# Linear attention inside a three-layer decoder kernel: sums G and folded weights M as fp16 high and low parts, with three fp16 products in place of one fp32 product

## The chip, the core and the metric

The kernel runs on one core of a Trainium2 chip. The core has a matrix engine (PE, TensorE), with its weight loads shown apart as PEld, a vector engine (DVE), a scalar engine (ACT), GpSimd (POOL) and a queue engine (SP) that issues DMA transfers. The metric is the device time in microseconds (us) of one whole execution.

## What is computed

128 sequences of 64 tokens, 128 wide, pass through linear attention, cross attention and a feed-forward layer, each followed by a layer norm. The change is in the linear attention, which the reference writes so (biases left out here):

```python
q_prime = exp(einsum('bnhd,df->bnhf', x @ Wq, wq_feat))          # 16 heads, 32 features
k_prime = exp(einsum('bnhd,df->bnhf', x @ Wk, wk_feat))
D_inv   = 1.0 / (einsum('bnhf,bhf->bnh', q_prime, k_prime.sum(axis=1)) + 1e-06)
context = einsum('bnhf,bnhd->bhfd', k_prime, x @ Wv)
out     = einsum('bnhf,bhfd,bnh->bnhd', q_prime, context, D_inv).reshape(b, n, H * DH) @ Wproj
```

The kernel regroups it. For a sequence b it forms G = x^T k_prime, which is 128 x 512 (all heads side by side). For each head h it multiplies the 32 columns of G by M_h = Wv_h Wproj_h, a 128 x 128 matrix that is folded once. The result C (128 rows of features for four heads at a time, four times 128 columns) is what q_prime, already scaled by D_inv, is multiplied with.

## The kernel before

The 128 sequences are worked in 16 groups of 8 (s = 0 to 15). All five engines run hand-written programs. Each walks through the same list of steps, PLAN, and does its own part of each step, so PLAN alone sets the order on every engine: HEAD is a prologue, PERIOD is one round of 86 steps that repeats 14 times with different groups in flight at once (`@2` is a step of the group two before), TAIL drains the rest. An engine executes in order: a step that waits holds up all that stands behind it on that engine.

The PE writes into eight banks of PSUM. Every step that needs a bank takes the next in rotation, so the step that stands eight bank uses later has to wait until this bank has been read out ("emptied"). Evictions are by ACT or DVE. For some steps a `+` in PLAN says that ACT does it, otherwise DVE.

The steps that matter here, for one group:

- `k0` to `k3`: k_prime for two sequences each. PE makes three fp16 products (L270 to L272), ACT takes exp into kp (L569). `q0` to `q3`: the same for q_prime into qT (L278 to L280, L576).
- `g0` to `g7`: G of one sequence. PE L320, one fp32 product of 64 rows by 512 columns (two records in the trace). It is copied out of its bank into one of four buffers GT: in PERIOD g0, g1 and g2 by ACT (L588, seen as L549) and the other five by DVE (L846). g4 to g7 reuse the buffers of g0 to g3, so their copies wait until c0 to c3 have been computed.
- `c0` to `c7`: C of one sequence. PE L330, 16 fp32 products, one for each head, with 32 columns of GT as the weights and 128 columns of Mh streamed. Four heads in turn go to the four 32-column strips of the array. One fp32 product is two matmul records and two weight-load records in the trace. C is copied into Cb, by ACT for c0, c4 and c7, by DVE for the others (L852).
- `ks`, `kst`, `dT`, `bc0` to `bc3`: the denominators. PE L287, L295, L305, L313. The step `dT` also needs DVE (De, Dv) and POOL (Dblk, L1056); `bc` scales qT on DVE (L838).
- `o0` to `o3`: PE L343 and L347, then DVE adds the residual (L860) and the layer norm follows: statistics (L867, L874) on DVE, `st1` to `st3` on POOL (L1061, L1064), `ap1` to `ap3` on DVE (L880).
- Cross attention: `kproj` and `qproj` evicted by ACT (L616, L620; L631, L633) and DVE (L887), `score` reduced to maxima by DVE (L897), `rows` (PE L409), `prob` (PE L421, L428; ACT L662), `pv` (PE L443; DVE L809), `oturn` (PE L451; DVE L905, L912), `cs` (a split into high and low parts by ACT L673 and POOL L1139, then a transposing DMA L1219), `proj` (PE L471 to L473; DVE L920).
- Feed-forward: `ap2` also splits x2 on POOL (L1090, L1092) for a transposing DMA; `up` (PE L491, L492; ACT Gelu L691), `stat` on DVE and POOL, `gs`, `gh`, `gl` (POOL L1106, ACT L709, POOL L1111), `down` (PE L511, L512; DVE L971).

In PERIOD the first half of G and C stands as `g0+ g1+ g2+ g3 ap2@3 down2@4 k3 ... prob0@2 prob1@2 st3@4 ap1@1 ap3@4 c0+ c1 pv0@2 ... c2`, the second half as `q2 cs1@2 oturn1@2 q3 g4 g5 g6 gs2@3 gl0@3 g7 gh1@3 qproj@1 gl1@3 kproj@1 c3 dT c4+ c5 c6 gs3@3 c7+ proj0@2 csplit proj1@2`.

## Time and profile before

| | |
|---|---|
| median of 3 runs | 674.9 us (671.55 to 675.94) |
| span of the profiled execution | 673.3 us |
| PE busy | 645.5 us (96%) |
| PEld busy | 455.3 us (68%) |
| DVE busy | 535.4 us (80%) |
| ACT busy | 437.5 us (65%) |
| POOL busy | 448.9 us (67%) |
| share of the chain that ended last: PE | 66% |
| same: POOL, DMA, DVE, issue, ACT | 12%, 8%, 6%, 4%, 2% |
| granted clock of the PE, mean | 0.997 |

Busy time counts the time in which at least one instruction of the engine was running. Matmuls overlap, so the number that matters for the PE is the distance from start to start, and an engine at 96% is not proved to be the limit by that number. The chain that ended last is followed back from the last instruction: at each step to what released it. "Idle before" and the brackets [... <-engine] in the rows give how long an engine stood still before an instruction and what it waited for.

### The profile page before, as it was taken

To read this page: it belongs to the slowest core of one execution; us is meant where nothing else is said; L and a number is where in the kernel's file an instruction comes from. 1 tells how busy PE (TensorE), PEld (TensorE's weight loads), DVE (VectorE), ACT (ScalarE), POOL (GpSimd) and SP (SyncE) were. 2 spreads that over 40 slices of the span, in tenths; PEclk is the share of its full clock that TensorE was granted. 3 is DMA by queue.
4 is the path that set the end of the run, shared out by engine and by line. 5 is a ranking of instruction groups with operands and counts; after the bars stand their busy time and mean duration, and the time that the engine had idled before them with its cause. 6 is when DMAs were issued, how large, how long until landed. Compare 5 with 4: busy or idle time off the path is not lost.

```text
span 673.3 us, 30461 instructions
## 1 busy us (share of the span) xinstructions
PE 645.5 (96%) x13160; PEld 455.3 (68%) x13160; DVE 535.4 (80%) x1485; ACT 437.5 (65%) x755; POOL 448.9 (67%) x495
## 2 busy tenths in 40 slices
PE   9999999999999989999999999999999999999684
PEld 6766767666766766676666667667666767667473
DVE  1656678788888878897788888878888888887787
ACT  3546465849578574947848494875849486777462
POOL 3233134867769586776959687795977779786652
PEclk9999999999999999999999999999999999999998
DMA  8102121262452434353343527336343634352300
GB/s 333 34 18 34 36 50 52 37 109 50 88 92 50 113 50 97 50 104 74 50 113 50 96 52 103 74 51 112 60 90 55 121 50 66 65 81 36 65 34 33
DMA packets 117816, 49.26 MB, mean 73 GB/s; under 512 B 108337, under 2 KB 108722, under 8 KB 117554
## 3 DMA queue, kind: packets, MB, share of 16 engines
q1 hardware_dynamic: 117682, 47.31, 36.7%
q8 instruction: 104, 1.70, 1.1%
q14 instruction: 30, 0.25, 0.1%
HBM read 16.88 MB, written 4.19 MB: 31 GB/s over the span
## 4 chain that ended last, share of the span: by engine, by line
PE 66%; POOL 12%; DMA 8%; DVE 6%; issue 4%; ACT 2%; SPq 2%; POOLq 0%; DVEq 0%
PE bank L330 12%; PE bank L347 7%; PE bank L320 6%; PE bank L443 4%; PE bank L428 4%; DMA cT<-cs 4%; PE bank L400 3%; POOL gall L1106 3%; DMA gT<-gs 2%; POOL rstd L1064 2%; PE bank L343 2%; DVE st L867 2%; PE bank L270 2%; PE bank L287 2%; PE bank L313 2%
## 5 line engine op out<-in xcount | busy, mean ns | idle before, releaser
L330 PEld LDWEIGHTS bank<-Mh,GT 128*32 128x32 f32 x4096 | 110.4, 110 | 23.9 <-issue 18.1
L330 PE MATMUL bank<-Mh,GT 128*32 128x128 f32 x4096 | 125.7, 273 | 0.5 <-issue 0.4
L897 DVE TENSOR_REDUCE mx<-bank 128x8 f32<-128x512 f32 x128 | 78.2, 682 | 13.4 <-PE bank L400 13.4
L1106 POOL TENSOR_TENSOR gall<-gall,lnr 128x512 f32<-128x512 f32 x56 | 71.3, 1283 | 20.7 <-DVE st L867 20.7
L846 DVE COPY GT<-bank 128x512 f32<-128x512 f32 x78 | 51.0, 688 | 36.3 <-PE bank L330 19.6
L662 ACT ACTIVATE PT<-bank 128x512 f32<-128x512 f32 x128 | 64.6, 622 | 14.1 <-PE bank L428 14.0
L1064 POOL TENSOR_TENSOR rstd<-ve,mhalf 128x4 f32<-128x4 f32 x64 | 66.6, 1041 | 5.3
L347 PE MATMUL bank<-Cb,qT 128*64 128x128 f32 x1024 | 67.2, 273 | 0.0
L1111 POOL TENSOR_TENSOR gs<-gall,gs 128x512 f16<-128x512 f32 x56 | 64.1, 1165 | 1.5 <-ACT gs L709 1.5
L320 PE MATMUL bank<-kp,xs 64*128 64x512 f32 x256 | 64.0, 616 | 0.0
L549 ACT ACTIVATE Mrow<-bank 64x128 f16<-64x128 f32 x16 | 4.3, 271 | 83.7 <-PE bank L409 83.7
L852 DVE COPY Cb<-bank 128x512 f32<-128x512 f32 x80 | 52.6, 673 | 7.6 <-PE bank L330 7.6
L347 PEld LDWEIGHTS bank<-Cb,qT 128*64 128x64 f32 x1024 | 58.4, 137 | 0.2 <-issue 0.2
L576 ACT ACTIVATE qT<-bank,qb 128x512 f32<-128x512 f32 x64 | 43.5, 683 | 12.1 <-PE bank L280 11.7
L880 DVE TENSOR_SCALAR x<-x,mv,rstd 128x128 f32<-128x128 f32 x128 | 49.6, 451 | 1.5 <-POOL rstd L1064 0.9
L1041 POOL TENSOR_TENSOR x<-x,bias 128x512 f32<-128x512 f32 x32 | 40.7, 1273 | 6.6 <-PE bank L481 4.4
L620 ACT ACTIVATE Kg<-bank,bkm,small 128x512 f32<-128x512 f32 x64 | 44.8, 801 | 0.0
L838 DVE TENSOR_TENSOR qT<-qT,bank 128x512 f32<-128x512 f32 x64 | 39.7, 682 | 6.2 <-PE bank L313 5.4
L569 ACT ACTIVATE kp<-bank 128x512 f32<-128x512 f32 x64 | 36.6, 597 | 11.9 <-PE bank L272 11.0
L867 DVE BATCH_NORM_STATS2 st<-gall 128x6 f32<-128x512 f32 x64 | 39.5, 680 | 5.2 <-ACT gall L691 5.0
L1027 POOL CAST xh<-xT 128x512 f16<-128x512 f32 x16 | 9.8, 610 | 50.6 <-DMA xT<-in_xT 50.6
L691 ACT ACTIVATE gall<-bank 128x512 f32<-128x512 f32 x64 | 33.4, 601 | 13.6 <-PE bank L492 13.6
(198 smaller groups left out, 1640.9 us busy)
## 6 DMA issues: line engine op xcount, KB each, us to landing
xT<-in_xT SPq DMA_DIRECT2D x16, 256.0 KB, 3.3
xs<-in_x_nat SPq DMA_DIRECT2D x16, 256.0 KB, 3.2
cxT<-in_cxT SPq DMA_DIRECT2D x16, 256.0 KB, 3.8
out_y<-yo SPq DMA_DIRECT2D x15, 256.0 KB, 2.0
Qm<-in_Wvp SPq DMA_DIRECT2D x1, 1024.0 KB, 7.4
gT<-gs SPq DMA_TRANSPOSE x56, 3.7
gall<-in_Wff SPq DMA_DIRECT2D x1, 768.0 KB, 10.0
small<-in_small SPq DMA_DIRECT2D x1, 523.0 KB, 8.6
```

The source lines that it names most:

```text
L320: e.matmul(bk[:, :], xs[s % 2][r0:r0 + 64, tile(t)], kp[r0:r0 + 64, tile(t, 512)], start=True, stop=True).then_inc(done, 1)
L330: m = e.matmul(bk[32 * j:32 * j + 32, tile(g_)], GT[b % 4][:, tile(hh, 32)], Mh[:, tile(hh)], start=True, stop=True)
L347: m = e.matmul(bk[64 * bb:64 * bb + 64, 0:128], qT[:, g_ * 512 + b * 64:g_ * 512 + b * 64 + 64], Cb[b][:, tile(g_)], start=False, stop=(g_ ...
L662: e.activation(PT[tp][:, tile(j, 512)], bank[uses["prob", s, i][0]][:, :], ACT.Exp, scale=SM).then_inc(emptied("prob", s, i)[0], 1)
L846: e.tensor_copy(GT[b % 4][:, :], bank[uses["g", s, b][0]][:, :]).then_inc(emptied("g", s, b)[0], 1)
L852: e.tensor_copy(Cb[b][:, :], bank[uses["c", s, b][0]][:, :]).then_inc(emptied("c", s, b)[0], 1)
L867: e.bn_stats(st[k][:, 6 * t:6 * t + 6], x[t]).then_inc(s_st[k], 1)
L880: e.tensor_scalar(x[:, tile(t)], x[:, tile(t)], mv[k][:, 2 * t:2 * t + 1], rstd[k][:, t:t + 1], ALU.subtract, ALU.mult).then_inc(s_ln[k], 1)
L897: e.tensor_reduce(mx[s % 2][:, c0:c0 + 8], bank[uses["score", s, i][0]][:, :].rearrange("p (n k) -> p n k", k=64), AX.X, ALU.max).then_inc ...
L1064: e.tensor_tensor(rstd[k][:, :], ve[k][:, :], mhalf[:, :], ALU.pow).then_inc(s_rstd[k], 1)
L1106: e.tensor_tensor(g[t][:, :], g[t][:, :], lnr[:, :], ALU.mult).then_inc(s_gs, 1)
L1111: e.tensor_tensor(gs[t % 2][:, 512:1024], g[t][:, :], gs[t % 2][:, 0:512], ALU.subtract).then_inc(s_gl, 1)
```

## The change

M is now kept as two fp16 matrices. ACT writes the bank times 16 (1/GS, GS = 1/16) into Mh, DVE writes the bank times 16 less Mh into Ml. G is kept the same way: for every g step ACT writes G/16 into one of four buffers Gh, and then DVE reads the same bank again and writes the remainder into Gl. The two scale factors cancel in the product. The bank is given free by DVE. So ACT now evicts all eight g of a group (three before) and DVE also works on all eight (five before), each after ACT. The wait for the buffer (`filled("c", ...)`) stands on ACT. The `+` after a g step no longer means anything; PLAN is not touched.

In cmat, 48 fp16 products take the place of 16 fp32 ones: for each set of four heads Gh by Mh, Gl by Mh and Gh by Ml, summed in PSUM.

```diff
-        Mh = sb("Mh", 2048)
+        Mh, Ml = sb("Mh", 2048, F16), sb("Ml", 2048, F16)
...
-                for hh in range(H):
-                    g_, j = hh // 4, hh % 4
-                    m = e.matmul(bk[32 * j:32 * j + 32, tile(g_)], GT[b % 4][:, tile(hh, 32)], Mh[:, tile(hh)], start=True, stop=True)
+                for g_ in range(4):
+                    for G, M in ((Gh, Mh), (Gl, Mh), (Gh, Ml)):
+                        for j in range(4):
+                            hh = 4 * g_ + j
+                            m = e.matmul(bk[32 * j:32 * j + 32, tile(g_)], G[b % 4][:, tile(hh, 32)], M[:, tile(hh)], start=(G is Gh and M is Mh), stop=(M is Ml))
                 m.then_inc(done, 1)
...
# ACT, gmat, now called for every g
-                copy("g", s, b, GT[b % 4][:, :])
+                w.wait_ge(*filled("g", s, b))
+                e.activation(Gh[b % 4][:, :], bank[uses["g", s, b][0]][:, :], ACT.Copy, scale=GS).then_inc(s_gth, 1)
...
# DVE, gmat, now called for every g
-                if b >= 4:
-                    w.wait_ge(*filled("c", s, b - 4))
-                elif s > 0:
-                    w.wait_ge(*filled("c", s - 1, b + 4))
-                w.wait_ge(*filled("g", s, b))
-                e.tensor_copy(GT[b % 4][:, :], bank[uses["g", s, b][0]][:, :]).then_inc(emptied("g", s, b)[0], 1)
+                w.wait_ge(s_gth, 8 * s + b + 1)
+                e.scalar_tensor_tensor(Gl[b % 4][:, :], bank[uses["g", s, b][0]][:, :], GS, Gh[b % 4][:, :],
+                                       ALU.mult, ALU.subtract).then_inc(emptied("g", s, b)[0], 1)
```

Three places show where the instructions stand. On ACT, at the second half of G in a steady round, before the change: the exp of q3, the high part gs1 of the feed-forward, and the evictions of qproj and kproj follow each other.

```order
L576 ACTIVATE qT<-bank5,qb 128x512 [waits s_bank5_full]
L709 ACTIVATE gs1<-gall 128x512 [waits s_g3_transposed,s_g_scaled]
L631 ACTIVATE Qu<-bank2,small2 128x512 [waits s_bank2_full]
L633 ACTIVATE Qm1<-bank2,bqm,small2 128x512 x2
L616 ACTIVATE Km1<-bank3,small2 128x512 [waits s_bank3_full]
L620 ACTIVATE Kg<-bank3,bkm,small2 128x512 x4
```

The same place after the change:

```order
L581 ACTIVATE qT<-bank5,qb 128x512 [waits s_bank5_full]
L594 ACTIVATE Gh0<-bank6 128x512 [waits s_bank6_full]
L594 ACTIVATE Gh1<-bank7 128x512 [waits s_bank7_full]
L594 ACTIVATE Gh2<-bank0 128x512 [waits s_bank0_full,s_bank2_full]
L594 ACTIVATE Gh3<-bank1 128x512 [waits s_bank1_full,s_bank4_full]
L715 ACTIVATE gs1<-gall 128x512 [waits s_g3_transposed,s_g_scaled]
L637 ACTIVATE Qu<-bank2,small2 128x512 [waits s_bank2_full]
L639 ACTIVATE Qm1<-bank2,bqm,small2 128x512 x2
L622 ACTIVATE Km1<-bank3,small2 128x512 [waits s_bank3_full]
L626 ACTIVATE Kg<-bank3,bkm,small2 128x512 x4
```

Four evictions now stand ahead of gs1 and the two projections, and the last (Gh3) also waits for bank4, the bank of c3, to be full.

On DVE, the same place before the change (GT0 to GT3 are g4 to g7, Qm1 is DVE's half of the qproj eviction):

```order
L912 TENSOR_TENSOR cn1<-bank4,rs1 128x16x2x8 [waits s_c_lo,s_rs]
L846 COPY GT0<-bank6 128x512 [waits s_bank6_full]
L846 COPY GT1<-bank7 128x512 [waits s_bank7_full]
L846 COPY GT2<-bank0 128x512 [waits s_bank0_full]
L846 COPY GT3<-bank1 128x512 [waits s_bank1_full,s_bank4_full]
L887 TENSOR_SCALAR Qm1<-bank2,small2 128x512 [waits s_Q_masked]
```

After it (this copy of the place has the bank numbers of another group):

```order
L922 TENSOR_TENSOR cn1<-bank7,rs1 128x16x2x8 [waits s_c_lo,s_rs]
L855 SCALAR_TENSOR_TENSOR Gl0<-bank1,Gh0 128x512 [waits s_G_hi]
L855 SCALAR_TENSOR_TENSOR Gl1<-bank2,Gh1 128x512 [waits s_G_hi]
L855 SCALAR_TENSOR_TENSOR Gl2<-bank3,Gh2 128x512 [waits s_G_hi]
L855 SCALAR_TENSOR_TENSOR Gl3<-bank4,Gh3 128x512 [waits s_G_hi]
L897 TENSOR_SCALAR Qm0<-bank5,small2 128x512 [waits s_Q_masked]
```

Four copies became four subtractions; what they wait for is now ACT.

On PE, one c step (c0 of a group) after the change. Before, it was one row of 16 products, `MATMUL bank<-Mh,GT 32x128 x16`. Here are its first seven rows, of which the last six are two of the four sets:

```order
L334 MATMUL bank5<-Mh,Gh0 32x128 [waits s_bank5_empty]
L334 MATMUL bank5<-Mh,Gh0 32x128 x3
L334 MATMUL bank5<-Mh,Gl0 32x128 x4
L334 MATMUL bank5<-Ml,Gh0 32x128 x4
L334 MATMUL bank5<-Mh,Gh0 32x128 x4
L334 MATMUL bank5<-Mh,Gl0 32x128 x4
L334 MATMUL bank5<-Ml,Gh0 32x128 x4
```

Each c step now has twelve rounds of four products; the four of a round go to four different strips of the array.

## Rows read from the trace of the kernel before

**Rows 1.** Windows: length; busy us of PE, PEld, DVE, ACT, POOL; clock, DMA.

```profile
107.60:574.20 466.60, 458.25 (x9703) 321.79 (x9701) 392.59 (x1081) 325.30 (x556) 353.22 (x383) 1.00 0.42 75
...
301.90:341.60 39.70, 38.57 (x812) 27.18 (x811) 32.60 (x91) 26.86 (x46) 29.39 (x32) 1.00 0.43 71
...
459.70:497.50 37.80, 37.80 (x813) 26.80 (x811) 32.53 (x92) 26.96 (x46) 29.08 (x32) 1.00 0.44 74
```

**Rows 2.** Timeline of PE, second half of C: start us, length us, instruction, count.

```profile
323.83 1.08 PE L330 MATMUL bank<-Mh,GT 128*32 128x128 f32 x32
324.73 1.08 PE L305 MATMUL bank<-qT,KSz 128*32 128x64 f32 x64
325.62 3.83 PE L330 MATMUL bank<-Mh,GT 128*32 128x128 f32 x128
329.38 0.23 PE L471 MATMUL bank<-xWh,cT 128*128 128x128 f16 x1
...
329.73 0.22 PE L471 MATMUL bank<-xWh,cT 128*128 128x128 f16 x1
```

**Rows 3.** Groups by line: instructions, busy us, mean ns of one, idle before.

```profile
L751 DVE TENSOR_TENSOR Wkfl<-bank,Wkfh 128x512 f16<-128x512 f32 x1 | 0.7, 692 | 6.9 <-ACT Wkfh L553 6.9
L887 DVE TENSOR_SCALAR Qm<-bank,small 128x512 f32<-128x512 f32 x32 | 24.4, 804 | 5.7 <-ACT Qm L633 5.7
L553 ACT ACTIVATE Wkfh<-bank 128x512 f16<-128x512 f32 x1 | 0.6, 597 | 6.3 <-PE bank L210 6.3
```

**Rows 4.** Timeline of DVE over one round.

```profile
304.21 0.69 DVE L846 COPY GT<-bank 128x512 f32<-128x512 f32 x1 [0.77 <-PE bank L320]
304.82 1.11 DVE L880 TENSOR_SCALAR x<-x,mv,rstd 128x128 f32<-128x128 f32 x4
...
310.71 1.12 DVE L880 TENSOR_SCALAR yo<-yo,mv,rstd 128x128 f32<-128x128 f32 x4 [0.91 <-POOL rstd L1064]
...
315.53 0.69 DVE L809 COPY OT<-bank 128x512 f32<-128x512 f32 x1 [1.24 <-PE bank L443]
316.70 2.47 DVE L867 BATCH_NORM_STATS2 st<-gall 128x6 f32<-128x512 f32 x4 [0.47 <-ACT gall L691]
...
321.12 0.42 DVE L912 TENSOR_TENSOR cn<-bank,rs 128x256 f32<-128x256 f32 x1
...
324.98 0.69 DVE L846 COPY GT<-bank 128x512 f32<-128x512 f32 x1 [1.35 <-PE bank L330]
...
336.30 4.88 DVE L897 TENSOR_REDUCE mx<-bank 128x8 f32<-128x512 f32 x8 [1.25 <-PE bank L400]
```

**Rows 5.** Timeline of ACT over the same round.

```profile
303.24 1.57 ACT L549 ACTIVATE GT<-bank 128x512 f32<-128x512 f32 x3 [0.72 <-PE bank L320]
...
321.58 0.42 ACT L673 ACTIVATE cs<-cn 128x256 f16<-128x256 f32 x1
321.91 0.67 ACT L576 ACTIVATE qT<-bank,qb 128x512 f32<-128x512 f32 x1
322.48 0.62 ACT L709 ACTIVATE gs<-gall 128x512 f16<-128x512 f32 x1
323.29 0.69 ACT L631 ACTIVATE Qu<-bank,small 128x512 f32<-128x512 f32 x1 [0.19 <-PE bank L376]
...
325.77 2.80 ACT L620 ACTIVATE Kg<-bank,bkm,small 128x512 f32<-128x512 f32 x4
```

**Rows 6.** Timeline of PE over the same round.

```profile
302.08 1.99 PE L320 MATMUL bank<-kp,xs 64*128 64x512 f32 x8
...
335.19 1.99 PE L400 MATMUL bank<-Kg,Qu 32*64 32x256 f32 x64 [0.20 <-ACT kp L569]
```

**Rows 7.** Timeline of POOL, the step ap2 and the root of st3.

```profile
305.99 0.61 POOL L1090 CAST x2s<-x 128x512 f16<-128x512 f32 x1 [0.96 <-DVE x L880]
...
309.56 1.12 POOL L1064 TENSOR_TENSOR rstd<-ve,mhalf 128x4 f32<-128x4 f32 x1
```

**Rows 8.** Who waited for whom: us in total, times, longest us.

```profile
PE bank L471 <- DMA cT<-cs: 5.5, 6, 1.7
```

More of the change, by code:

```diff
@@ L557, in mh @@
                     o = Mh[:, :].rearrange("p (c k a n) -> p c k a n", c=2, k=4, a=2)[:, c // 2, :, c % 2, :]
-                    copy("mh", 0, c, o, shape="p (k n) -> p k n")
+                    w.wait_ge(*filled("mh", 0, c))
+                    e.activation(o, bank[uses["mh", 0, c][0]][:, :].rearrange("p (k n) -> p k n", k=4), ACT.Copy, scale=1 / GS).then_inc(s_mhh, 1)
             def nbeta_():
@@ L756, in xw, with mh @@
                 e.tensor_tensor(xWl[:, :], xWall, xWh[:, :], ALU.subtract).then_inc(s_xwl, 1)
+            def mh(c2):
+                for c in range(2 * c2, 2 * c2 + 2):
+                    hi, lo_ = [v[:, :].rearrange("p (c k a n) -> p c k a n", c=2, k=4, a=2)[:, c // 2, :, c % 2, :] for v in (Mh, Ml)]
+                    w.wait_ge(s_mhh, c + 1)
+                    e.scalar_tensor_tensor(lo_, bank[uses["mh", 0, c][0]][:, :].rearrange("p (k n) -> p k n", k=4), 1 / GS, hi,
+                                           ALU.mult, ALU.subtract).then_inc(emptied("mh", 0, c)[0], 1)
             def sel_():
```

18 lines of the change are left out of this document (12 added, 6 removed).

## The prediction, made before the changed kernel was run

> **What bounds the kernel now.** I read the windows first. Between 107.6 and 574.2 us twelve rounds repeat, 466.6/12 = 38.9 us each, and the PE is busy in 458 of those 467 us [rows 1]. One round (459.7 to 497.5) has the PE busy for all of its 37.8 us; I take that as the PE's own work in a round, so an average round holds 1.1 us of stray PE waits. In the same stretch DVE is busy 392.6/12 = 32.7 us a round and ACT 27.1. So the PE is the bound, and a shorter PE program shortens the kernel only until another chain of waits is longer. The second view is the timeline of one round (301.9 to 341.6), engine by engine, because it shows how far the others are from being the bound: DVE stands still for 1.24 us before the pv copy, 1.35 us before the last g copy and 1.25 us before the score maxima, each time for the PE [rows 4].
>
> **PE: the c steps.** Four c steps in a row start at 325.62 and the next step starts at 329.38: 3.76/4 = 0.94 us each, and the single one before them took 324.73 - 323.83 = 0.90 [rows 2]. That is 32 matmul records of 128 columns in 0.90 us, 28 ns a record, where four records of different strips run side by side. New: 48 records, each with half the work of an old record (one pass over 128 fp16 columns; an fp32 record makes two passes, which I read from the row of L305: 64 records of 64 fp32 columns take 325.62 - 324.73 = 0.89 us, 13.9 ns each, half as long for half the columns). 128 columns once are as much as 64 columns twice, so 13.9 ns x 48 = 0.67 us; with the same small loss between steps 0.69. A c step gains 0.90 - 0.69 = 0.21 to 0.25 us, I take 0.22; 8 in a round gain 1.8 us, 128 in the kernel 28 us. Bounds: no better than 0.25 x 128 = 32 us; at the other end, if a record costs 28 ns whatever it does, a c step takes 48 x 28 = 1.34 us and loses 0.44.
>
> The Trainium skill, TensorEngine Tiling, section Instruction Overhead, puts about 60 cycles on every matmul, however short; at 2.4 GHz 48 of them would be an estimated 1.2 us a step, a loss of 0.3 where the row gives a gain. The row of L305, 13.9 ns a record in this same four-strip form, disagrees with that rule as a floor for tiled matmuls, and the sum goes by the row.
>
> **ACT and DVE: durations.** The low part on DVE reads PSUM and an fp16 tile and writes fp16. The nearest row is the same split of a weight, L751, 692 ns [rows 3] against 0.69 us for the plain copy [rows 4]; the dearest form, with two scalar columns, took 804 ns [rows 3]. Mine has a constant, so 0.69; back to back such instructions start every 0.60 us (eight in 4.88) [rows 4]. ACT's fp16 eviction is 597 ns [rows 3], and three in a row start every 0.49 us [rows 5]. Per round ACT does five more (2.5 us), DVE three more (1.8 us). DVE goes to 34.5 us of work, ACT to 29.6, the PE to 37.8 - 1.8 = 36.0. By work alone the PE would still be the bound and the kernel would be 28 us shorter. But the new work is in chains, and I walk one round to see what is late next. I hold the PE's g0 at 302.08 [rows 6].
>
> 1. First half of G. ACT copies from 303.24, now four: done at 303.24 + 3 x 0.49 + 0.60 = 305.3, just when it used to start the exp of k3, so ACT loses nothing. DVE begins at 303.9 (first high part done, and it was idle), subtracts four times by 0.60, and is free at 306.3. Before, it had one copy and began ap2 at 304.82 [rows 4]. DVE is 1.46 us late.
> 2. ap2 feeds POOL, which did nothing else then: it had waited 0.96 us for it [rows 7]. Its split, bias and root run in series to 309.56 + 1.12 = 310.68, and DVE waited 0.91 us for that before ap3 [rows 4]. All of it moves by 1.46: ap3 starts at 312.17. Five copies later (c1, OT, KS, c2, OT) DVE reaches the statistics at 312.17 + 1.04 + 5 x 0.60 = 316.2, against 316.70. The 1.24 us for which it waited for pv swallow the delay, since the PE is not behind: prob1 starts 0.55 late (its banks wait for down3 on DVE) and three c steps give 0.66 back. From here to the last cn DVE was busy throughout: cn ends at 321.0 instead of 321.54.
> 3. ACT: cs1 at 321.1, q3 at 321.4, then the four high parts from 322.0, step 0.49. The last waits for c3. With the PE about 1.3 us ahead by then (up no longer waits for a late pv, and the c steps are shorter), c3 is full near 323.4 and ACT reaches that copy at 323.45: no wait. gs1 at 323.95, Qu at 324.5 instead of 323.29 [rows 5], all evictions of the projections 1.2 us late, and the bank of kproj is free at 329.8 instead of 325.77 + 2.80 = 328.57.
> 4. PE: it would reach proj at 326.7, with c4 to c7 done. proj0 waits for the transposed cT and for DVE's share of qproj's bank (about 328.1); it waited for that DMA 6 times already [rows 8], and the same POOL and DMA work still stands ahead of it. proj1 waits for kproj's bank, 329.85. So about 3 us of PE waits take the place of the 1.8 us saved, and of the other time that the PE had won.
> 5. From the start of proj1 to score the PE took 335.19 - 329.73 = 5.46 us [rows 2, 6]; about 0.36 of it were waits, 0.20 for the exp of k0 [rows 6] and the rest my reading of small gaps at down and score, and both go since ACT and the DMAs are relatively earlier. So score starts at 329.85 + 5.10 = 334.95, 0.24 earlier than in this round, and the maxima on DVE with it.
>
> The round closes 0.24 us earlier than this one did, which was 39.70 us [rows 1]: 39.46. That is 0.58 more than the average of 38.88. Now DVE, POOL, ACT, and the PE from proj to o, are one ring: a stray delay on it counts, where the PE alone had 1.1 us. This round already has the usual ones of DVE and POOL in it; I allow 0.2 us more. **Sum:** 12 x (0.58 + 0.2) = +9.4 us. The c steps of the first two groups (before 107 us) stand where DVE and ACT have little to do: 2 x 1.8 = -3.6 us. In the last 99 us I give nothing either way: the gain of two groups' c steps against 3 more DVE instructions each. 673.3 + 9.4 - 3.6 = 679.1 us for the profiled execution, whose span is 1.6 us under the median of the runs: 680.7. I say 680.
>
> **Rivals.** *The PE stays the bound* (faster). For it: I count ACT's and DVE's work at its place in one round that happened to be long; if one of the waits in steps 1 to 3 is covered more than I think, each us off the ring is a us off the round until the PE's 36.0. Against it: the ring has no large slack left that I can find. All the way it is 645 us; halfway (a ring of 37.8 us) it is 673.3 - 12 x 1.1 - 3.6 = 656.5, and 658 for the runs.
>
> *ACT stands at the last high part* (slower). If the PE is not ahead at c3, so that it is full at 325.0 as before and not at 323.4, ACT's g7 copy ends at 325.6, all evictions behind it come another 1.6 us late, proj1 too, and the round is 39.5 + 1.6 = 41.1: 2.2 + 0.2 over the average, 12 x 2.4 - 3.6 = +25, or 700 for the runs. It decides from the point where c3 is full later than 323.45 on this clock. For it: the PE's lead of 1.3 us at g4 comes mostly from waits, not from work. Half as late gives 690.
>
> *The small matmuls cost a slot each* (slower; the change then does not do what it says). At 28 ns a record the PE needs 37.8 + 8 x 0.44 = 41.3 us a round, 2.4 over the average in 12 rounds, and 3.5 in each of the four groups at the ends: 673.3 + 29 + 14 = 716. In rows: this needs L305 to be no guide for fp16. With the 60 cycles of the Trainium skill's rule it would be about 702 as an estimate.
>
> **Chances.** My forecast (a ring of 39.0 to 40.2 us, 671 to 689 by the same sum) 0.55; the PE or a shorter ring 0.20; ACT's stand 0.20; slots 0.05. About 1% is what a measurement of this kernel can tell from no change, 668 to 682. The faster rival lies below that but for its upper end, 0.18. Slower takes the last two and a third of the forecast, 0.42. The same: 0.40. Range: 662 to 695 leaves out the lower half of the first rival (0.1) and the far end of the slow ones (0.1).
>
> **What would show it.** c steps of about 0.67 to 0.69 us from start to start; the low part on DVE at 0.69 us, the high part at 0.60. DVE starts ap2 about 4.2 us after the PE's g0 (2.74 before). PE waits of 2 to 3 us a round at proj (L475 to L477 of the new file), released by ACT's Kg or the cT DMA, where there were none or little; PE busy near 90%. If PE stays at 96% and the c steps are short, the ring was shorter than I counted. If c steps take over 0.9 us, the slots rival holds. If ACT idles before Gh for the PE's c, it is ACT's stand. What would make it wrong most easily is step 2, the order in which DVE's wait for pv and POOL's chain cover each other, since the whole delay of 1.46 us is hidden there.

## The result, and the profile after

The changed kernel takes **727.3 us** (median of 4 runs, 725.2 to 729.1) against 675.4 us for the kernel before on the same chip. The ratio is 1.079, 95% interval 1.076 to 1.082. It is slower by 52 us where I had predicted 680 and a range that ended at 695. The chip has a second, slower state that some executions fall in, and all times and ratios below are of the others.

| | before | after |
|---|---|---|
| span of the profiled execution | 673.3 us | 725.3 us |
| PE busy, matmuls | 645.5 us (96%), 13160 | 634.7 us (88%), 15208 |
| DVE busy, instructions | 535.4 us (80%), 1485 | 566.2 us (78%), 1539 |
| ACT busy, instructions | 437.5 us (65%), 755 | 473.6 us (65%), 833 |
| start to start over 12 rounds | 466.6 / 12 = 38.88 us | 504.8 / 12 = 42.07 us |
| ahead of these rounds | 107.6 us | 119.1 us |
| behind them | 99.1 us | 101.4 us |
| granted clock of the PE, mean | 0.997 | 0.994 |

Of the 52 us, 38.2 come from the twelve rounds, 11.5 from the stretch ahead of them and 2.3 from the end. The window over the twelve rounds, in the columns of [rows 1]:

```profile
119.10:623.90 504.80, 449.40 (x11239) 306.30 (x11237) 413.69 (x1117) 352.83 (x616) 353.90 (x383) 1.00 0.39 70
```

Against the first row of [rows 1], the PE's busy time fell by 8.9 us in twelve rounds, less than half of the 12 x 1.8 = 21.6 that I had predicted. And the PE now stands still for 504.8 - 449.4 = 55.4 us, 4.6 us a round, where it stood still for 8.4 us in all. The granted clock of this window is 1.00, so it is not a slower clock. Who is waited for stands in the waits (us in total, times, longest):

```profile
PEld bank L334 <- issue: 62.2, 87, 2.2
DVE Gl L855 <- ACT Gh L594: 41.2, 47, 2.5
PE bank L334 <- issue: 35.8, 27, 2.0
ACT Gh L594 <- PE bank L334: 16.8, 17, 2.4
PEld bank L475 <- ACT Kg L626: 9.0, 9, 1.5
```

L334 is the c step, L594 ScalarE's high part, L855 VectorE's low part, L626 the eviction Kg, L475 the step proj. The largest PE wait is not for another engine. "Issue" means that nothing in the profile released it. Before, the weight loads of the c step had stood 18.1 us in this way, and its matmuls 0.4. The groups by line show that each new operation lasts as long as I had taken it to (busy us, mean ns; then idle before):

```profile
L855 DVE SCALAR_TENSOR_TENSOR Gl<-bank,Gh 128x512 f16<-128x512 f32 x128 | 81.3, 685 | 41.3 <-ACT Gh L594 41.2
L334 PE MATMUL bank<-Mh,Gh 128*32 128x128 f16 x2048 | 94.7, 220 | 14.9 <-issue 13.1
L594 ACT ACTIVATE Gh<-bank 128x512 f16<-128x512 f32 x128 | 68.1, 602 | 34.7 <-PE bank L322 17.7
```

**Inside the c steps.** The PE's timeline in the round that begins with g0 at 413.18 us, from the second (c5) of four c steps in a row back to back to the end of the fourth (c7) (start us, length us, instruction, count, idle before):

```profile
437.97 0.23 PE L334 MATMUL bank<-Mh,Gh 128*32 128x128 f16 x4
438.03 0.23 PE L334 MATMUL bank<-Mh,Gl 128*32 128x128 f16 x3
...
439.42 0.23 PE L334 MATMUL bank<-Mh,Gl 128*32 128x128 f16 x1 [1.16 <-issue]
439.42 0.28 PE L334 MATMUL bank<-Ml,Gh 128*32 128x128 f16 x4
...
441.10 0.27 PE L334 MATMUL bank<-Ml,Gh 128*32 128x128 f16 x4
441.16 0.23 PE L334 MATMUL bank<-Mh,Gh 128*32 128x128 f16 x3
...
443.43 0.23 PE L334 MATMUL bank<-Mh,Gh 128*32 128x128 f16 x1 [2.05 <-issue]
...
443.71 0.23 PE L475 MATMUL bank<-xWh,cT 128*128 128x128 f16 x1
```

Groups of four matmuls start 0.055 us apart, and then, in the middle of a group of four whose operands have long been there, the engine stops for 1.16 and for 2.05 us. Nothing has a semaphore there. The c steps c4 to c7 need 192 x 13.9 ns = 2.7 us when nothing is in the way. Here they take from 437.30 to 443.71, 6.4 us, 1.6 each.

The clue is in where it stops. I counted the PE's instructions (weight loads and matmuls) from the start of the program. The four matmuls of this round after which it stops inside a step have the numbers 18161, 18416, 18926 and 19182: 255, 510 and 256 apart. The profile's DMA part has a queue that carries instructions. This is its row before, after, and in two experiments of the next section (e7 has 32 PE instructions in a c step where before has 64 and after 96; e4 has 128):

```profile
q8 instruction: 104, 1.70, 1.1%
```

```profile
q8 instruction: 120, 1.97, 1.1%
```

```profile
q8 instruction: 88, 1.44, 1.0%
```

```profile
q8 instruction: 136, 2.23, 1.2%
```

Blocks of 1.70 MB / 104 = 16 KB. With two instructions to a matmul the four programs have 26320, 30416, 22224 and 34512 PE instructions. Divided by 256 that is 102.8, 118.8, 86.8 and 134.8, each time 1.2 blocks less than the row: one block is 256 PE instructions. In the trace's DMA records the blocks of the round above start at 420.60, 424.11, 428.08, 436.69, 440.71 and 445.52. The stops end at 422.96, 426.52, 439.42 and 443.43, 2.4 to 2.7 us behind the start of a block. Two starts are never less than 3.29 us apart in the whole run (3.24 in the kernel before). With 3.4 us to a block, near the shortest, the PE is given an instruction every 13.3 ns, or 27 ns for a matmul with its weight load. **A c step of 96 instructions is then given in 1.28 us, though it is done in 0.67.** In the round above the blocks are further apart, 3.97 and 4.02 us, which makes 15.7 ns an instruction and 1.5 us a step, near the 1.6 that c4 to c7 take. Before, a c step had 64 instructions, given in 0.85 us at 3.4 us a block and done in 0.90 [rows 2]: just supplied. That is the reading that I had missed.

### The profile page after: what moved, and what is told of

It is laid out like the page before. It is cut to its first block, busy times and chain, and to the rows that moved or that the text cites. A ratio compares the mean times of both kernels' runs of the same rounds, so it can differ in the third digit from the quotient of the medians.

```text
span 725.3 us, 34692 instructions
## 1 busy us (share of the span) xinstructions
PE 634.7 (88%) x15208; PEld 436.6 (60%) x15208; DVE 566.2 (78%) x1539; ACT 473.6 (65%) x833; POOL 449.5 (62%) x495
## 4 chain that ended last, share of the span: by engine, by line
PE 65%; DVE 11%; ACT 9%; issue 9%; POOL 4%; DMA 1%; SPq 0%; POOLq 0%; DVEq 0%; ACTq 0%
PE bank L334 9%; PE bank L351 7%; PE bank L322 6%; PE bank L447 4%; DVE Gl L855 4%; PE bank L404 4%; ACT Kg L626 3%; PE bank L315 2%; PE bank L432 2%; PE bank L347 2%; PE bank L289 2%; PE bank L455 2%; PE bank L272 2%; ACT Qm L639 2%; DVE x L890 2%
## 5 line engine op out<-in xcount | busy, mean ns | idle before, releaser
L855 DVE SCALAR_TENSOR_TENSOR Gl<-bank,Gh 128x512 f16<-128x512 f32 x128 | 81.3, 685 | 41.3 <-ACT Gh L594 41.2
L334 PE MATMUL bank<-Mh,Gh 128*32 128x128 f16 x2048 | 94.7, 220 | 14.9 <-issue 13.1
L334 PE MATMUL bank<-Ml,Gh 128*32 128x128 f16 x2048 | 94.4, 219 | 13.7 <-issue 13.7
L334 PE MATMUL bank<-Mh,Gl 128*32 128x128 f16 x2048 | 93.9, 219 | 9.0 <-issue 9.0
L594 ACT ACTIVATE Gh<-bank 128x512 f16<-128x512 f32 x128 | 68.1, 602 | 34.7 <-PE bank L322 17.7
L334 PEld LDWEIGHTS bank<-Mh,Gh 128*32 128x32 f16 x2048 | 62.8, 97 | 33.2 <-issue 32.1
L334 PEld LDWEIGHTS bank<-Ml,Gh 128*32 128x32 f16 x2048 | 63.5, 97 | 15.6 <-issue 15.5
L334 PEld LDWEIGHTS bank<-Mh,Gl 128*32 128x32 f16 x2048 | 62.8, 97 | 14.5 <-issue 14.5
L447 PE MATMUL bank<-PT,Vblk 128*32 128x64 f32 x2048 | 39.2, 220 | 12.3 <-issue 11.8
```

Source lines behind the costliest of these rows:

```text
L334: m = e.matmul(bk[32 * j:32 * j + 32, tile(g_)], G[b % 4][:, tile(hh, 32)], M[:, tile(hh)], start=(G is Gh and M is Mh), stop=(M is Ml))
L447: m = e.matmul(bk[32 * j:32 * j + 32, tile(2 * g_ + t2, 64)], V3[s % 2][:, 32 * tp + 16 * t2 + hh, :], PT[tp][:, c0:c0 + 64], start=True, ...
L594: e.activation(Gh[b % 4][:, :], bank[uses["g", s, b][0]][:, :], ACT.Copy, scale=GS).then_inc(s_gth, 1)
L855: e.scalar_tensor_tensor(Gl[b % 4][:, :], bank[uses["g", s, b][0]][:, :], GS, Gh[b % 4][:, :], ALU.mult, ALU.subtract).then_inc(emptied("g ...
```

## The experiments

Rounds are counted from the step `rows` of one group to the next, over the same twelve rounds. "Stops" are the distances of two matmuls of one step that are 0.15 us or more over the usual one with no wait between them, counted between 105 and 700 us, and their sum in us; where nothing stands I did not count. "PE instr." is the number of PE instructions in a c step. Each ratio is to runs of the kernel before that were made together with that kernel's (medians 673.9 to 676.3 us).

| kernel | us | ratio [95%] | round | stops, sum | PE instr. | evictions of G |
|---|---|---|---|---|---|---|
| before | 675.4 | 1 | 38.88 | 3, 2.1 | 64 | one |
| after | 727.3 | 1.079 [1.076, 1.082] | 42.06 | 35, 44.4 | 96 | two |
| e1_high_product_only | 711.9 | 1.054 [1.047, 1.061] | 41.21 | 11, 10.9 | 32 | two |
| e2_products_without_evictions | 711.3 | 1.054 [1.049, 1.058] | 40.98 | 36, 49.7 | 96 | one |
| e3_evictions_without_products | 707.8 | 1.050 [1.045, 1.054] | 41.09 | 10, 7.1 | 64 | two |
| e4_fp32_products_cut_in_two | 766.0 | 1.136 [1.129, 1.143] | 45.16 | 47, 72.8 | 128 | one |
| e5_c_steps_spread | 743.4 | 1.101 [1.094, 1.107] | 43.84 | 11, 11.2 | 96 | one |
| e6_weights_split_only | 674.2 | 0.998 [0.995, 1.001] | 39.00 | 24, 24.9 | 64 | one |
| e7_one_fp16_product | 666.7 | 0.988 [0.983, 0.994] | 38.45 | 8, 7.2 | 32 | one |
| e8_last_g_behind_projections | 727.8 | 1.075 [1.071, 1.079] | 42.71 | | 64 | two |
| e9_first_half_evictions | 685.4 | 1.017 [1.013, 1.021] | 39.76 | 11, 7.4 | 64 | two for g0 to g3 |
| e10_second_half_evictions | 698.1 | 1.035 [1.030, 1.039] | 40.29 | 5, 4.2 | 64 | two for g4 to g7 |
| e11_one_product_shorter_ring | 676.4 | 1.005 [1.000, 1.011] | 39.67 | | 32 | one |
| e12_before_shorter_ring | 676.2 | 1.003 [0.999, 1.006] | 38.83 | 7, 3.6 | 64 | one |
| e13_before_pool_ring_shorter | 706.6 | 1.043 [1.040, 1.047] | 41.38 | 9, 6.9 | 64 | one |
| e14_one_product_pool_ring_shorter | 710.1 | 1.050 [1.045, 1.054] | 41.99 | | 32 | one |
| e15_after_pool_ring_shorter | 746.5 | 1.101 [1.096, 1.106] | 43.86 | 38, 50.4 | 96 | two |

### The parts of the change apart

**e1** keeps the evictions and leaves out the two low products:

```diff
-                    for G, M in ((Gh, Mh), (Gl, Mh), (Gh, Ml)):
+                    for G, M in ((Gh, Mh),):
```

> The changed kernel with one product in a c step (Gh by Mh) in place of three; both low products are left out, while ACT and DVE still make all high and low parts. The PE executes 32 instructions (weight loads and matmuls) a c step, where the changed kernel has 96 and the kernel before 64. Theory A, instruction supply: in the changed kernel the PE stands still inside its c steps because its instructions arrive in blocks of 256 no faster than one in 3.47 us (13.6 ns an instruction); with 32 instructions that ends, no step has a gap inside it, and what is left is the ring of ACT, DVE and POOL of the prediction. If that ring is 39.1 us a round as I counted, 670 to 680 us; if it has slack, down to 640. Theory B, the ring alone costs the 50 us: about 720 still. Theory C, an fp16 product in four strips is slow by itself (a slot each): in between, about 675, with c steps of 0.45 us.

**e2** keeps the three products' form and count, but G is evicted once, as before, and all three use the same tiles (the low parts are left out):

```diff
-                    for G, M in ((Gh, Mh), (Gl, Mh), (Gh, Ml)):
+                    for n in range(3):
...
-                e.scalar_tensor_tensor(Gl[b % 4][:, :], bank[uses["g", s, b][0]][:, :], GS, Gh[b % 4][:, :], ...
+                e.tensor_scalar(GT[b % 4][:, :], bank[uses["g", s, b][0]][:, :], 2.0 ** -4, None, ALU.mult) ...
```

> The kernel before with its own evictions (one fp16 copy of G, by the engine that did it before; M as one fp16 copy) and 48 fp16 products a c step, three times the same pair, so that the PE does exactly what it does in the changed kernel while ACT and DVE do what they did before (the sum is three times the high product, no low parts). Theory A: the gaps inside c steps are all there, 690 to 720 us. Theory B: the PE gains 0.22 us a c step and nothing else changes, 645 to 655 us. Theory C: c steps are long evenly, not by gaps; about 700.

**e3** is the opposite: the changed evictions, and on the PE the program of the kernel before, one fp32 product, of the remainder (the high product is left out):

```diff
-        Gh, Gl, Cb = [sb(f"Gh{i}", 512, F16) for i in range(4)], [sb(f"Gl{i}", 512, F16) for i in range(4)], ...
+        Gl, Cb = [sb(f"Gl{i}", 512) for i in range(4)], ...
+        Gh = [v[:, 256:512].bitcast(F16) for v in Gl]
...
-                    for G, M in ((Gh, Mh), (Gl, Mh), (Gh, Ml)):
+                    for G, M in ((Gl, Mh),):
```

> The changed evictions of G (ACT writes a high part for all eight, then DVE works on all eight, the wait for the buffer on ACT) with the PE program of the kernel before, 16 fp32 products a c step. DVE writes the low part as fp32 and the PE multiplies that (M is one fp32 copy as before), so the high product is left out. Theory B, the ring with the PE late at c3: a round of 41 us, about 700 us or more. Theory A: the PE's own work and its instruction supply are those of before, and the evictions cost what is not hidden: 675 to 690.

Measured: the products alone cost 2.10 us a round (e2), the evictions alone 2.21 (e3), and both together 3.18. Counted in the traces from the start of one matmul to the start of the next, the c steps take 8.26 us a round in e2 and 8.27 after, against 7.25 before, and the pv steps, which follow c steps and were not changed, 3.19 and 2.94 against 2.13. For e2 these two make up 2.07 of its 2.10 us.

So there are **two losses of about the same size**, and they cover each other for 1.1 us: a PE that is held up comes later to the place where it would have waited for ScalarE. I read this overlap from the shrunken waits (below, step 4) and not from a run of its own. The stretch ahead of the rounds ends at 117.6 us in e2 and 111.7 in e3, against 107.6 before and 119.1 after. The 11.5 us lost there are thus mostly the products': that is where c steps stand close together and little else runs.

The share of the evictions is a plain chain. e3's ScalarE and PE in one round, whose g0 is at 400.91 us:

```profile
423.53 0.60 ACT L594 ACTIVATE Gl<-bank 128x512 f16<-128x512 f32 x1 [0.94 <-PE bank L335]
...
427.01 2.81 ACT L626 ACTIVATE Kg<-bank,bkm,small 128x512 f32<-128x512 f32 x4
```

```profile
428.49 0.22 PE L478 MATMUL bank<-xWl,cT 128*128 128x128 f16 x1
429.87 0.23 PE L476 MATMUL bank<-xWh,cT 128*128 128x128 f16 x1 [1.17 <-ACT Kg L626]
```

The last high part (g7) stands and waits for c3, which must have freed its tile. Behind it stand the evictions of the projections, the last of them Kg, which frees the bank of kproj, and PE's proj1 waits for that. In each of the twelve rounds ScalarE waits 0.9 us there (10.7 us in twelve), and the PE then waits for Kg, 13.7 us in twelve. This is the rival that I had called "ACT stands at the last high part": it had the last high part end 1.6 us late, at 325.6 on the prediction's clock, and e3's ends at 325.3. It said a round of 41.1, and e3's is 41.09, but that the two agree so closely is in part luck: the rival put all of its 2.2 us on the second half of G, and e9 and e10 below find 0.88 us for the first half and 1.41 for the second.

e1 has in a c step half the PE instructions of e3, with the same evictions, and its round is the same, 41.21, where I had expected 670 to 680 us in all. Its PE is not the bound: it is busy for 86% of the span. It no longer waits at c3, and in the round that is looked at below, at step 5, it gives about 1.4 us back to a slower clock. That this holds for every round I have not shown.

### Is it the supply of instructions?

**e4** takes the kernel before and cuts each fp32 product of 128 columns in two of 64, nothing left out. The columns to be multiplied are the same, the instructions twice as many:

```diff
-                    m = e.matmul(bk[32 * j:32 * j + 32, tile(g_)], GT[b % 4][:, tile(hh, 32)], Mh[:, tile(hh)], start=True, stop=True)
+                        for n in range(2):
+                            m = e.matmul(bk[32 * j:32 * j + 32, 128 * g_ + 64 * n:128 * g_ + 64 * n + 64], GT[b % 4][:, tile(hh, 32)], ...
```

> The kernel before with one edit: each fp32 product of a c step (128 columns) is cut in two of 64 columns. The columns streamed and all results are the same, but a c step has 128 PE instructions in place of 64. Nothing changes on ACT and DVE. Theory A: 128 x 13.6 ns = 1.74 us a c step when the supply binds, against 0.90: gaps inside c steps at multiples of 256 instructions, 710 to 760 us. Theories B and C: 64-column fp32 records take 13.9 ns each in L305, so a c step stays at 0.90 us, 675 us.

It is the slowest kernel of all, 766 us and 45.16 a round, 6.3 over before and more than the 710 to 760 us expected. The c steps take 11.83 us a round from start to start, 4.58 more than before, and the pv steps 1.20 more. In its timeline the stops stand as they do after:

```profile
416.54 0.84 PE L332 MATMUL bank<-Mh,GT 128*32 128x64 f32 x45
418.78 1.99 PE L332 MATMUL bank<-Mh,GT 128*32 128x64 f32 x128 [1.39 <-issue]
422.52 0.69 PE L332 MATMUL bank<-Mh,GT 128*32 128x64 f32 x34 [1.75 <-issue]
```

They come after the instructions 18694, 18950, 19460 and 19716: 256, 510 and 256 apart. The 128 matmuls between two stops are 256 instructions, one block.

**e5** is e2 with the c steps spread over the round, so that they no longer follow each other closely (low parts left out, as in e2):

```diff
-k0 k1 ... k3 down3@4 ab2@3 q0 prob0@2
-prob1@2 st3@4 ap1@1 ap3@4 c0+ c1 pv0@2 ... q3 g4 ... c3 dT c4+ c5 c6 gs3@3 c7+ proj0@2 csplit proj1@2 vproj@1 xb gh2@3 ...
+k0 k1 ... k3 c0+ down3@4 ab2@3 q0 c1 prob0@2
+prob1@2 st3@4 ap1@1 ap3@4 pv0@2 ... q3 g4 ... c3 dT c4+ gs3@3 proj0@2 csplit proj1@2 c5 vproj@1 xb c6 gh2@3 ... bc1 c7+ bc2
```

> The run e2 (48 products a c step three times the same pair, the evictions of the kernel before) with nothing changed but places in the repeating part of the plan: c0, c1, c2 and c5, c6, c7 no longer stand in a row beside pv and dT but between steps with few and long instructions (k, q, up, proj, vproj, bc). Number and kind of all instructions are the same on every engine. Instruction supply: the blocks of 256 can now be fetched while the PE works, most gaps inside steps go, and of the 37 us that e2 is over the kernel before most come back: 660 to 685 us. If the gaps belong to the products and not to how dense they stand, it stays at 711, or is worse because evictions are out of their tuned places.

The stops fall from 36 (49.7 us) to 11 (11.2 us), with the same 96 instructions in a c step. That is what the supply says and what a cost in each matmul would not. The time did not follow, though: 743.4 us where 660 to 685 was expected, and slower than e2. The evictions of the c banks now stand where VectorE is needed for other things (it waits 43.8 us for the PE's c steps, 7.6 in the kernel before, and GpSimd 88.4 us for VectorE's statistics, 38.3 before). So the stops speak for the cause, the time by itself does not, and the spreading is no remedy.

**e6** splits only the weights: two fp16 products, G in a single fp16 part (G's low part left out), evictions as before. It has as many PE instructions as the kernel before, and half of its columns in the c step:

```diff
+                for g_ in range(4):
+                    for n, M in enumerate((Mh, Ml)):
...
+                            m = e.matmul(bk[32 * j:32 * j + 32, tile(g_)], GT[b % 4][:, tile(hh, 32)], M[:, tile(hh)], start=(n == 0), stop=(n == 1))
```

> The kernel before with M as fp16 high and low parts (split once in the prologue), G as one fp16 copy made by the engine that made it before, and two fp16 products a c step, 64 PE instructions as in the kernel before (the low part of G is left out). By columns a c step is half as long, 0.45 us, and a round has 3.6 us less PE work. Without a supply limit: about 645 us. With one (256 instructions take at least 3.47 us): c4 to c7 have the 256 instructions they always had and still need about 3.5 us, against 3.6 before; 660 to 675 us, and the gaps inside steps are back.

**e7** has one fp16 product (all low parts left out), evictions as before:

```diff
-        Mh = sb("Mh", 2048)
+        Mh = sb("Mh", 2048, F16)
...
-        GT, Cb = [sb(f"GT{i}", 512) for i in range(4)], ...
+        GT, Cb = [sb(f"GT{i}", 512, F16) for i in range(4)], ...
```

> The kernel before with G and M each as one fp16 copy, made by the engines that made them before, and one fp16 product for each head: 32 PE instructions a c step, no low parts at all. Supply no longer binds (half the instructions), the evictions are those of before, so the PE work falls by 8 x 0.67 = 5.4 us a round to 32.4. What stops it then is the ring of before, which by the walk of the prediction without its two added pieces (1.46 and 1.85 us) is 36 us a round: 635 to 650 us. If the round stays over 38.5 us, the ring was long already and my count of it was wrong.

e6 changes nothing that can be measured, 0.998. It has 24 stops, 24.9 us in all, where before had 3, 2.1 us. But the supply is not all that holds it: its c steps, from start to start and without waits, take 5.1 us a round where before had 7.25, its pv steps 2.8 for 2.13, and its PE waits 14.5 us for cT in the twelve rounds (4.5 before). e7, with a half of the instructions, has few stops and is 1.2% faster, and no more than that (666.7 us for 635 to 650 expected), though its PE is busy for only 407.6 of 453.0 us. What holds it is another chain, and the next experiments look for it.

### The ring beside the PE

In e7 the chain that ended last runs, in a piece of one round, like this (start us, us, what):

```profile
347.79 0.61 ACT gall L693
348.42 0.71 DVE st L869
349.20 2.16 POOL gall L1108 x2
...
352.08 1.02 POOL rstd L1066
...
355.80 1.32 POOL cs L1141 x2
357.12 1.51 SPq L1221
358.73 2.49 DMA cT<-cs
```

From the evictions of up through the statistics, GpSimd, the split of cn and its transposing DMA to proj: the PE waits there for cT 24 times, 35.9 us. I took it for a ring of 38.4 us that must have been in the kernel before too, under the PE's 37.8 us of work.

**e8** is e3 with the eviction of g7 moved, on ScalarE behind Kg and on VectorE behind c5, so that no one waits for c3 ahead of the projections (high product left out, as in e3):

```diff
-            for name, s, t, on_act in PLAN:
+            for name, s, t, on_act in moved(PLAN, ("kproj", 1, 0)):
```

> The run e3 (changed evictions, fp32 products) with one order changed: in each full round the eviction of g7 stands behind the evictions of kproj on ACT (not ahead of gs1), and on DVE behind the copy of c5. PE, POOL and SP are untouched. If ACT's stand for c3 and the g7 copy itself are on the ring, the projections' banks are free 1.06 + 0.48 = 1.5 us earlier and a round takes 39.5 instead of 41.1 us: about 690 us. If it is not on the ring, 707 as in e3.

It gained nothing: 727.8 us where about 690 was expected and e3 had 707.8. The wait goes to the PE's c7, which now needs a low part that comes late:

```profile
PEld bank L347 <- DVE Gl L860: 37.5, 15, 3.0
```

**e9 and e10** split e3 in two, with the new evictions only for g0 to g3, or only for g4 to g7 (`NEW` is then 4 to 7):

```diff
+    NEW = (0, 1, 2, 3)
...
+                if b not in NEW:
+                    copy("g", s, b, Gl[b % 4][:, :], scale=GS)
+                    return
```

> TensorE's program of the kernel before (no fp16 products of G); only g0 to g3 are evicted the new way (high part on ScalarE, remainder on VectorE), g4 to g7 once, as before. The high product of c0 to c3 is left out. With both halves the new way (e3_evictions_without_products) the round was 41.09 us. Theory: TensorE does not bound this, the ring does, and e7 puts the ring of the kernel before at about 38.4 us. The first half of G adds four VectorE remainders of 0.69 us to what was two evictions, 1.46 us ahead of ap2: round 39.9 us, span about 686 us. If instead only ScalarE's wait for c3 had made the 41.1, this kernel, which has none, stays at the 38.9 us round and 675 us.

> The complement: g0 to g3 evicted as before, g4 to g7 the new way, TensorE's program that of the kernel before; the high product of c4 to c7 is left out. ScalarE then has four high parts of 0.60 us and g7's wait ahead of Kg instead of two copies, and waits for the bank of c3. Theory: about 39.1 to 39.6 us a round, 680 to 685 us. If ScalarE's wait for c3 alone made the 41.1 us of e3_evictions_without_products: 41 us and 708 us here, too.

e9 takes 685.4 us where 686 was expected, and 39.76 a round where 39.9 was. I had worked out 1.46 us more work in the chain, and 0.88 arrive in the round, so by this estimate the chain of the kernel before had 0.6 us of room: it was 38.3 us long. e10 missed its number (698.1 for 680 to 685), since I had counted ScalarE's two more instructions, 1.0 us, and too little of its wait:

```profile
ACT Gl L598 <- PE bank L336: 19.7, 18, 2.7
...
PEld bank L477 <- ACT Kg L630: 17.3, 13, 1.4
```

The first of these rows has six waits outside the twelve rounds; inside them it is 11.3 us, 0.94 a round. With 1.0 that makes 1.9 us on ScalarE's path for 1.41 in the round, 0.5 us of room, which puts that path at 38.4, an estimate too. Both take it that all of the added time lay in the chain. The two halves add up, 0.88 + 1.41 = 2.29 for e3's 2.21. The second half is the dearer.

**e11 and e12** give three evictions, the last of g0 to g3, c1 and ks, from VectorE to ScalarE; e11 in e7, e12 in the kernel before:

```diff
-... g0+ g1+ g2+ g3 ap2@3 ... c0+ c1 pv0@2 x1s@1 ab1@1 ks gs0@3 ...
+... g0+ g1+ g2+ g3+ ap2@3 ... c0+ c1+ pv0@2 x1s@1 ab1@1 ks+ gs0@3 ...
```

> e7_one_fp16_product (one fp16 product a step, 32 instructions instead of 64; low parts left out; 38.45 us a round) with three evictions, g3, c1 and ks, given from VectorE to ScalarE, which idles there. If the ring through VectorE's first half of G, POOL, cn, the DMA of the statistics, Kg and the scores was the bound of e7, the ring shortens by 1.3 + 0.6 + 0.6 us: round about 36, span 635 to 650 us. If TensorE or its instruction supply was the bound, it stays at 38.4 us and 667 us.

> The kernel before, nothing left out, fp32 products, with the same three evictions g3, c1 and ks given to ScalarE. The ring shortens to about 36 us, and TensorE, busy 37.8 us of the 38.9 us round, becomes the bound: round about 37.8 to 38, span 657 to 665 us. If TensorE bounded the kernel before already, as the prediction read it: no change, 675 us.

Both miss: e12 is the same as before, and e11 is 1.2 us a round slower than e7. No change is what e12 had for the case that the PE is the bound of the kernel before, and e12 alone does not speak against that. The chain of e11 shows another reason:

```profile
353.23 2.10 ACT PT L664 x4
355.33 0.22 ACT Cb L551
355.62 0.69 ACT Cb L551
...
357.32 1.22 ACT L693
358.62 0.61 ACT gall L693
```

ScalarE sits in the same ring. Its exponentials of prob, the copies behind them and the load of the next function table stand ahead of gall, and in e7 the PE had released gall, not ScalarE's own row of work. I had taken 2.5 us from one half of the ring and put 1.5 of it into the other. The clock may have done a part of it too (mean 0.937 for e7's 0.956). So the work of VectorE and that of ScalarE on this ring seem to be near each other; no run measures by how much they differ.

**e13, e14 and e15** shorten GpSimd's part alone, in the kernel before, in e7 and in the changed kernel. gs1, which e7's chain has ahead of the statistics, goes behind the split of cn:

```diff
-... ks gs0@3 c2 gs1@3 pv1@2 stat@3 ... cs1@2 oturn1@2
+... ks gs0@3 c2 pv1@2 stat@3 ... cs1@2 oturn1@2 gs1@3
```

> The kernel before, nothing left out, with one change of order on GpSimd alone: gs1 (the second product with the gains, 1.27 us) behind the split of cn instead of ahead of the statistics of the last layer norm, so that the statistics, cn's split and the transposed cT come about 1.0 us earlier each round. If the path GpSimd - DMA - proj bounds some of the rounds (theory: ring of 38.4 us beside a TensorE program of 37.8 us): round 38.9 to about 38.3 us, span 664 to 669 us. If TensorE or the path through ScalarE is the bound: no change, 673 to 676 us.

> e7_one_fp16_product (one fp16 product a step, low parts left out, 666.7 us, 38.45 us a round) with the same change of order on GpSimd. Theory: there the chain of waits runs through GpSimd, the DMA of cT and proj in every round, and e11 lengthened ScalarE's half of the same ring, which is why it gained nothing. Then this one gains up to 1.0 us a round: 37.5 to 37.9 us, 655 to 660 us. If the supply of TensorE's instructions or its clock held e7: no change, 667 us.

> The changed kernel, nothing left out, with the same change of order on GpSimd. Theory: its rounds of 42.06 us are bounded by TensorE with the gaps in its c and pv steps and by the wait for ScalarE's Kg, not by cT: no change, 725 to 729 us. If the ring through GpSimd and cT still carries it: up to 12 us less, 715 us.

All three are slower, by 2.5, 3.5 and 1.8 us a round, and for a reason that I had put in myself. ScalarE's gh1 stands right ahead of the evictions of the projections and needs gs1. In e13:

```profile
ACT gs L709 <- POOL gall L1106: 45.0, 12, 3.8
```

That is 3.75 us in each round, and the chain that ended last goes from it over Kg to proj1. So they don't answer what I asked. They do show that ScalarE's path to Kg presses: 3.75 us of wait on it go with 3.5 us more in e7 (where the same wait is 44.7 us in all), and with 2.5 in the kernel before. A part of both may be the clock, whose mean fell from 0.956 to 0.920 in e14 and from 0.997 to 0.985 in e13. In the changed kernel ScalarE comes later by itself and waits only 12.0 us for gs1, 1.0 a round, and the round is 1.8 longer. All three had been expected to be faster or unchanged. The ring is not out of the way in the changed kernel either, and I have no measurement of how the 3.2 us of the change would fall apart further.

## Why the prediction was wrong, and where it was right

**The sum.** It had +9.4 us for the twelve rounds, -3.6 ahead of them and nothing behind them. Measured were +38.2, +11.5 and +2.3. A round was to take 39.46 + 0.2 us and takes 42.06. Two steps failed: the PE's gain in the c steps, and "no wait" at the last high part in step 3.

**What bounds the kernel now.** I read the PE as the bound with 1.1 us of stray waits. By the windows it stands still for 8.35 / 12 = 0.70 us a round; the other 0.4 is the difference between its shortest round and the average one. Of the 8.35 us, 6.1 are waits for the DMAs of cT and gT, so a chain beside the PE is nearly as long. The estimates from e9 and e10 put it at 38.3 and 38.4 us beside 37.8 us of PE work: two bounds with half a microsecond between them. "I can find no large slack" was right.

**The c steps.** 0.67 us with no pause was right: c0 and c1 take 421.90 - 420.55 = 1.35 us together.

```profile
420.55 0.24 PE L334 MATMUL bank<-Mh,Gh 128*32 128x128 f16 x4
...
421.90 0.39 PE L447 MATMUL bank<-PT,Vblk 128*32 128x64 f32 x11
```

**The failed term** is the next one, "A c step gains 0.90 - 0.69 = 0.21 to 0.25 us, I take 0.22; 8 in a round gain 1.8 us". The c steps of a round lost 1.0 us (8.27 for 7.25 from start to start), and the pv steps, at which I had put nothing, 0.8. I priced matmuls by what the array needs and forgot what has to bring them there: 96 instructions at 13.3 ns, 1.28 us, in a run of steps. The row that I leaned on, L305 with 64 matmuls in 0.89 us [rows 2], has 128 instructions in 0.89 us, 7 ns each. It shows what the PE does with instructions that were fetched ahead, and not what it can keep up. These run out where such steps follow each other, and that is what c4 to c7 do behind L305. Priced by the supply at 3.4 us a block, a c step in a run of them loses 1.28 - 0.90 = 0.38 us where I let it gain 0.22. Eight such steps would be an estimated 3.0 us a round; e2 measured 2.1, half of it in the pv steps. c0 and c1, which stand as a pair, were supplied in the round above.

The rival "the small matmuls cost a slot each" priced a c step at 1.34 us by 28 ns a matmul, which is near 1.28, for another reason. It gave 716, and I gave it 0.05, since L305 spoke against a cost in each matmul. It does: e5 has the same matmuls and 11 stops for 36. The Trainium skill, TensorEngine Tiling (Array Packing), section Instruction Overhead, gives every matmul about 60 cycles, 25 ns at 2.4 GHz. The steps in which nothing stops do not bear that out for the four-strip form: they take 13.9 ns a matmul, and no run here shows 25 ns as a cost of the matmul itself.

**Steps 1 to 5.** The walk through one round held where the PE did, and e1 is the run to read it in, since its c steps are short and its stops few. In its round with g0 at 361.13, that is 59.05 us behind the round of the prediction, VectorE and ScalarE read:

```profile
365.40 1.11 DVE L890 TENSOR_SCALAR x<-x,mv,rstd 128x128 f32<-128x128 f32 x4
...
371.29 1.12 DVE L890 TENSOR_SCALAR yo<-yo,mv,rstd 128x128 f32<-128x128 f32 x4 [0.91 <-POOL rstd L1078]
...
375.31 2.46 DVE L877 BATCH_NORM_STATS2 st<-gall 128x6 f32<-128x512 f32 x4
...
379.73 0.42 DVE L922 TENSOR_TENSOR cn<-bank,rs 128x256 f32<-128x256 f32 x1
```

```profile
381.08 2.29 ACT L594 ACTIVATE Gh<-bank 128x512 f16<-128x512 f32 x4
...
386.25 2.81 ACT L626 ACTIVATE Kg<-bank,bkm,small 128x512 f32<-128x512 f32 x4
```

Step 1 had ap2 at 306.3 (365.35 on this clock). Step 2 had ap3 at 312.17 (371.22), the statistics at 316.2 (375.25) and cn's end at 321.0 (380.05), and step 3 the high parts from 322.0 (381.05) and kproj's bank free at 329.8 (388.85). The rows have 365.40, 371.29, 375.31, 380.15, 381.08 and 389.06. In this round, of a kernel with short c steps, the delay of 1.46 us was swallowed where I had said. In e9, with the c steps of the kernel before, it was not: the first half alone lengthened the average round by 0.88 us.

Step 3 failed in the changed kernel and in e3, in its words "c3 is full near 323.4 and ACT reaches that copy at 323.45: no wait". It rested on a PE that is 1.3 us ahead. In e3 it isn't ahead, and in the changed kernel the stops in pv and c hold it back: the last high part starts at 436.63, 23.45 us behind g0, where I had 21.4.

```profile
436.63 0.60 ACT L594 ACTIVATE Gh<-bank 128x512 f16<-128x512 f32 x1 [0.70 <-PE bank L334]
```

Step 4 had "about 3 us of PE waits" at proj for Kg or cT. Those for Kg are 9.0 us in the whole run by the weight loads and not 36, because the PE itself is late: it gets to proj0 at 443.71, 30.5 us behind g0, where I had let it arrive after 24.6.

Step 5, proj1 to score in 5.10 us, held in the changed kernel: proj1 starts at 444.05 and the score at 449.17, 5.12 later. In e1 it failed. The score starts at 395.58 and not at 394.0, 6.47 us behind proj1. After waits of 2.77 and 1.18 us at proj the PE's matmuls are spaced twice as far apart, with a granted clock of 0.51 from 388.6 to 392.1:

```profile
387.42 0.23 PE L475 MATMUL bank<-xWh,cT 128*128 128x128 f16 x1 [2.77 <-DVE Qm L897]
...
389.11 0.29 PE L475 MATMUL bank<-xWh,cT 128*128 128x128 f16 x1 [1.18 <-ACT Kg L626]
...
389.30 0.31 PE L477 MATMUL bank<-xWl,cT 128*128 128x128 f16 x1
```

**Rivals and range.** The rival that I gave 0.20, ACT's stand, came true for the evictions: e3 has its wait and its 41.1 us a round. The range left its end out and knew nothing of the supply, which is worth as much again. Both losses lay on the side to which I had given 0.42.

## What to carry to other kernels

Count the instructions of a step as well as its columns: here, with a weight load for each matmul of 128 columns or less, a run of small steps was bound by how fast instructions arrive, and less PE work in more and shorter matmuls lost. The sign in the profile was PE time "<-issue" in the middle of a step, at distances of 256 instructions, with a block on the queue that carries instructions shortly ahead of its end. When a new eviction must wait for a tile that a later step of the other engine frees, price what stands behind it on its engine, and do not take credit for an engine that is ahead when the same change may hold it back.

## What the runs showed of the hardware

The supply: 256 PE instructions in a block of 16 KB, block starts at least 3.23 us apart in every run (3.29 in the changed kernel), and 2.2 to 2.9 us from a block's start to the first instruction that had waited for it. Of the changed kernel's distances between 100 and 700 us, 15 are under 3.6 us and 20 are 3.9 to 4.3, as in the c steps shown above. There the transposing DMAs were at work too; that they make the difference is not shown. The average of a round is far from this limit: before, 813 matmuls are 6.4 blocks, 22 us of 38.9.

The clock: the kernels whose PE had less work and longer waits had a lower mean clock, and gave back part of what they had won. In e7 the PE waited 2.20 us for cT up to 359.95, and the clock fell at 360.4, in the next wait for cT, of 0.91 us (length; busy us of PE, PEld, DVE, ACT, POOL; clock, DMA):

```profile
361.30:363.40 2.10, 2.05 (x22) 1.89 (x22) 1.29 (x6) 0.00 (x0) 1.52 (x2) 0.50 1.05 195
363.40:367.30 3.90, 3.90 (x14) 1.20 (x14) 2.14 (x7) 2.83 (x5) 3.46 (x5) 0.50 0.17 33
367.30:372.00 4.70, 4.70 (x101) 3.31 (x101) 3.06 (x7) 1.37 (x3) 3.01 (x3) 1.00 0.32 64
```

The granted clock of 0.50 is the lower of the two levels, 1.2 GHz, up to 367.3, and 1.00 the upper, 2.4 GHz. The mean over the span was 0.956 in e7, 0.940 in e1 and 0.937 in e11, against 0.997 in the kernel before. A part of e7's round of 38.45 us is therefore the clock and not the ring, so that e7 alone does not measure the ring. That is why the 38.3 and 38.4 us above are taken from e9 and e10, whose clock was 0.992.

What stays open: which of the paths of the ring, through GpSimd and cT or through ScalarE and Kg, is the longer one in the kernel before. e11 to e15 moved each of them at the cost of the other. A kernel that is faster than before at full precision was not found.
